# Attention with a single pass over the keys: which engines copy the transposed outputs and add them up, and where in a pair's rounds its products stand

## The reference

```
q = M @ Wq.T;  k, v = split(x @ Wkv.T + bkv)
sim = q k^T / 8, masked;  attn = softmax(sim);  out = attn @ v
out = out @ Wo.T + bo;  m = layer_norm(out + M)
z = layer_norm(relu(m @ W1.T + b1) @ W2.T + b2 + m)
```

## Time and profile before

| | |
|---|---|
| median of 3 runs | 712.91 us (712.37 to 714.04) |
| the profiled execution, device time | 711.92 us |
| its span | 710.1 us |
| mean granted TensorE clock | 0.977 of full speed |
| TensorE busy | 633.1 us, 89% |
| VectorE busy | 552.7 us, 78% |
| ScalarE busy | 363.8 us, 51% |
| GpSimd busy | 245.5 us, 35% |
| DMA | 128.37 MB, mean 181 GB/s |

### The profile page before, as it was taken

One profiled execution on the slowest core, in us unless ns is written; L12 is line 12 of the kernel. 1 busy time (PEld: TensorE's weight loads), 2 busy tenths in 40 slices (PEclk: granted clock), 3 DMA queues, 4 the chain that ended last, 5 costly groups with the idle time before them and its releaser, 6 DMA issues.

```text
span 710.1 us, 11125 instructions
## 1 busy us (share of the span) xinstructions
PE 633.1 (89%) x3382; PEld 398.3 (56%) x3382; DVE 552.7 (78%) x688; ACT 363.8 (51%) x658; POOL 245.5 (35%) x305
## 2 busy tenths in 40 slices
PE   3967999999999999998999999999998287899995
PEld 3755556555556556554565566555564144688883
DVE  5378899989998999988998999899989345433333
ACT  5355566556665566654666555566564212433332
POOL 3212552246322632264225522463221601522223
PEclk9999999999999999999999999999999699899998
DMA  7038788988898889888797998888887960023311
GB/s 281 1 77 221 201 213 208 240 204 214 206 242 205 199 220 252 201 199 203 193 239 192 215 228 228 200 215 211 199 203 197 285 166 30 30 89 95 107 64 60
DMA packets 54938, 128.37 MB, mean 181 GB/s; under 512 B 15840, under 2 KB 19424, under 8 KB 54624
## 3 DMA queue, kind: packets, MB, share of 16 engines
q1 hardware_dynamic: 44128, 101.97, 56.1%
q10 hardware_dynamic: 10752, 25.70, 13.8%
HBM read 23.80 MB, written 1.05 MB: 35 GB/s over the span
## 4 chain that ended last, share of the span: by engine, by line
PE 42%; DVE 21%; SPq 14%; issue 9%; DMA 7%; ACT 3%; ACTq 2%; DVEq 1%; POOL 1%; POOLq 0%
SPq L350 14%; DVE st L679 11%; PE tail L853 9%; PE slot L825 8%; PE slot L904 6%; PE slot L912 6%; DMA pt<-st 6%; DVE prob L669 6%; PE slot L750 5%; PE tail L750 5%; ACT prob L531 2%; ACTq L567 2%; PE tail L860 1%; DMA wq_raw<-in_wq 1%; PE slot L784 1%
## 5 line engine op out<-in xcount | busy, mean ns | idle before, releaser
L531 ACT ACTIVATE prob<-prob,negmax 128x896 f32<-128x896 f32 x224 | 233.6, 1043 | 215.1 <-DVE negmax L669 192.6
L669 DVE CUSTOM_DVE_ANT_0 prob<-slot,lower,negmax_old 128x896 f32<-128x896 f32 x224 | 248.9, 1148 | 40.6 <-PE slot L825 28.3
L679 DVE STREAM_TRANSPOSE st<-prob 128x1792 f32<-128x1792 f32 x112 | 228.4, 2040 | 15.0 <-DMA pt<-st 14.6
L853 PE MATMUL tail<-pt,val 128*64 128x512 f32 x784 | 185.2, 606 | 17.2 <-DMA pt<-st 10.8
L853 PEld LDWEIGHTS tail<-pt,val 128*64 128x64 f32 x784 | 51.7, 138 | 113.4 <-issue 105.1
L825 PE MATMUL slot<-k_hi,q_hi 64*128 64x448 f32 x448 | 95.7, 416 | 19.5 <-DVE negmax L669 16.1
L825 PEld LDWEIGHTS slot<-k_hi,q_hi 64*128 64x128 f32 x448 | 44.0, 185 | 87.0 <-issue 77.7
L825 PE MATMUL slot<-k_hi,q_lo 64*128 64x448 f32 x448 | 85.4, 366 | 0.0
L825 PE MATMUL slot<-k_lo,q_hi 64*128 64x448 f32 x448 | 84.8, 364 | 0.0
L429 POOL TENSOR_TENSOR total<-total,alpha 128x8 f32<-128x8 f32 x28 | 5.8, 206 | 199.2 <-ACT alpha L571 199.2
L442 POOL TENSOR_TENSOR k_lo<-k_raw,k_hi 128x896 fp32r<-128x896 f32 x27 | 57.1, 2114 | 3.9 <-POOL k_hi L439 0.2
(11 more groups left out here) (112 smaller groups left out, 812.6 us busy)
## 6 DMA issues: line engine op xcount, KB each, us to landing
pt<-st SPq DMA_DIRECT2D x672, 112.0 KB, 3.1
pt<-st ACTq DMA_DIRECT2D x224, 112.0 KB, 3.4
w_raw<-in_w SPq DMA_DIRECT2D x32, 256.0 KB, 2.8
x_raw<-in_x SPq DMA_DIRECT2D x13, 448.0 KB, 4.0
mask_raw<-in_mask SPq DMA_DIRECT2D x7, 448.0 KB, 4.5
mt_raw<-in_mt SPq DMA_DIRECT2D x2, 512.0 KB, 7.6
wq_raw<-in_wq SPq DMA_DIRECT2D x2, 512.0 KB, 8.2
wo_raw<-in_wo SPq DMA_DIRECT2D x1, 1024.0 KB, 5.1
```

Of the source, the lines that this page charges most:

```text
L531: nc.scalar.activation(unit, unit, ACT.Exp, bias=negmax[:, p, u:u + 1], scale=-1.0, accum_out=psumrow[:, p, u:u + 1]).then_inc(exp_done, 1)
L669: nc.vector.tensor_tensor_reduce(out=prob[:, i % 2, h].rearrange("p (b n) -> p b n", b=2), in0=slot[:, j, :, :HALF], in1=lower[:, i].rearr ...
L679: nc.vector.transpose(st[:, g].rearrange("p b k (t i) -> p k b t i", t=2)[:, :, :, t2], prob[:, i % 2].rearrange("p h (k b i) -> p (h k) b ...
L853: last = nc.tensor.matmul(outT[DH * h:DH * h + DH], val[:, val_at(i, parity ^ (p < 0)), head(p, h)], moving, start=(i == 0), stop=(i == KT ...
```

## The change

ScalarE copies `tp` into `outT_sb` after F (its part of A, a new semaphore `f_copied`), and GpSimd adds `outT_sb` to `acc`. VectorE does nothing in A. Since `outT_sb` now holds both copies in turn, C waits until the add before has been done (the last C still waits for F alone). `tp_free` waits for `f_copied` where it waited for the add. For the last two pairs, in the tail, VectorE keeps its add straight from PSUM, as a step "+".

The table ROUNDS is new: F and A stand in round 0 of every pair; W3 goes behind K; V products move to rounds 2 and 3 in pairs 0 and 1; in pair 2, V5 stands behind F and two W in round 0, and all five others of the W in round 2; ScalarE's copies of V1 to V4 stand between the two exponentials.

```
@@ -50,22 +50,22 @@
 
 
 ROUNDS = (
-    ('S E0 E1 W0 W1 W2 W3 X M1 R0',
-     'S P0 E0 V1 E1 Z K H L X B1',
-     'S E0 E1 F W4 W5 W6 C A X M0 Q',
-     'S E0 E1 V2 X B0'),
-    ('S E0 E1 W0 W1 W2 W3 X M1',
-     'S E0 V3 E1 Z K H L X B1',
-     'S E0 E1 F W4 W5 W6 C A X M0',
-     'S E0 E1 V4 X B0'),
-    ('S E0 V5 E1 W0 W1 X M1',
+    ('S F E0 A E1 W0 W1 W2 X M1 R0',
+     'S P0 E0 E1 Z K H L W3 X B1',
+     'S E0 V1 E1 W4 W5 W6 C X M0 Q',
+     'S E0 V2 E1 X B0'),
+    ('S F E0 A E1 W0 W1 W2 X M1',
+     'S E0 E1 Z K H L W3 X B1',
+     'S E0 V3 E1 W4 W5 W6 C X M0',
+     'S E0 V4 E1 X B0'),
+    ('S F E0 A E1 W0 W1 V5 X M1',
      'S E0 V6 E1 Z K H J0 L X B1',
-     'S E0 E1 F W2 W3 W4 A X R1 M0',
-     'S E0 E1 W5 W6 C X B0 J1 I'),
-    ('S E0 E1 W0 W1 W2 W3 X M1',
-     'S E0 E1 Z F K H L A X B1',
+     'S E0 E1 W2 W3 W4 W5 W6 C X R1 M0',
+     'S E0 E1 X B0 J1 I'),
+    ('S F E0 A E1 W0 W1 W2 X M1',
+     'S E0 E1 Z K H L W3 X B1',
      'S E0 E1 W4 W5 W6 C X M0',
-     'S E0 E1 N0 X B0 O'),
+     'S E0 N0 E1 X B0 O'),
 )
 
 
@@ -110,9 +110,9 @@
         out.extend([("X", b, 3), ("M", b, 1), ("B", b, 1), ("Z", b, 0)])
         out.extend([("G", 0, 0), ("T", 0, 0), ("D", 0, 0)])
         out.extend([*(("W", a, kt) for kt in range(3)), ("G", 1, 0), ("T", 1, 0), ("D", 1, 0)])
-        out.extend([*(("W", a, kt) for kt in range(3, KT)), ("C", a, 0), ("Y", 0, 0), ("F", a, 0), ("A", a, 0), ("N", a, 0)])
+        out.extend([*(("W", a, kt) for kt in range(3, KT)), ("C", a, 0), ("Y", 0, 0), ("F", a, 0), ("+", a, 0), ("N", a, 0)])
         out.extend([("Y", 0, 1), ("Y", 0, 2), ("Y", 0, 3), ("G", a, 0), ("T", a, 0), ("D", a, 0)])
-        out.extend([*(("W", b, kt) for kt in range(KT)), ("C", b, 0), ("Y", 1, 0), ("F", b, 0), ("A", b, 0), ("N", b, 0)])
+        out.extend([*(("W", b, kt) for kt in range(KT)), ("C", b, 0), ("Y", 1, 0), ("F", b, 0), ("+", b, 0), ("N", b, 0)])
         out.extend([("Y", 1, 1), ("Y", 1, 2), ("Y", 1, 3), ("G", b, 0), ("T", b, 0), ("D", b, 0)])
         out.extend([("Y", 2, t) for t in range(QT)])
     return out
@@ -218,7 +218,7 @@
         xposed = sem("xposed")
         landed = [sem(f"landed{b}") for b in range(4)]
         v_filled, v_copied = sem("v_filled"), sem("v_copied")
-        f_filled, acc_added = sem("f_filled"), sem("acc_added")
+        f_filled, f_copied, acc_added = sem("f_filled"), sem("f_copied"), sem("acc_added")
         pv_done = sem("pv_done")
         outT_copied = sem("outT_copied")
         acc_scaled = sem("acc_scaled")
@@ -432,6 +432,12 @@
                         if is_past(n, PAIRS):
                             pool.wait_ge(acc_added, n - PAIRS + 1)
                         nc.gpsimd.tensor_tensor(by_head(acc[:, own]), by_head(acc[:, own]), per_head(alpha, own), ALU.mult).then_inc(acc_scaled, 1)
+                    if kind == "A":
+                        copied, own = in_register(pool, pair_no(c, p) + 1), acc[:, p % PAIRS].rearrange("p t n -> p (t n)")
+                        pool.wait_ge(zeroed, 2)
+                        pool.wait_ge(acc_scaled, copied)
+                        pool.wait_ge(f_copied, copied)
+                        nc.gpsimd.tensor_tensor(own, own, outT_sb[:], ALU.add).then_inc(acc_added, 1)
                     if kind == "L":
                         copied, done = in_register(pool, keys_use(pair_no(c, p)) + 1), in_register(pool, pair_no(c, p))
                         pool.wait_ge(zeroed, 2)
@@ -546,10 +552,15 @@
                                              ACT.Identity, bias=bk_sb[:, p % PAIRS:p % PAIRS + 1]).then_inc(drained[KEYS_RING], 1)
                     if kind == "C":
                         act.wait_ge(pv_done, KT * (n + 1))
-                        if is_past(n, 1):
+                        if isinstance(n, int) and n == PAIRS * CHUNKS - 1:
                             act.wait_ge(f_filled, n)
+                        elif is_past(n, 1):
+                            act.wait_ge(acc_added, n)
                         nc.scalar.copy(outT_sb[:].rearrange("p (g t a i) -> p g a t i", g=2, a=QUAD, t=2),
                                        outT.rearrange("p (g a t i) -> p g a t i", g=2, a=QUAD, t=2)).then_inc(outT_copied, 1)
+                    if kind == "A":
+                        act.wait_ge(f_filled, n + 1)
+                        nc.scalar.copy(outT_sb[:], tp).then_inc(f_copied, 1)
                     if kind == "T":
                         act.wait_ge(aoT_filled, p + 1)
                         nc.scalar.activation(ao2[0][:, p], gather_bank(p), ACT.Identity, bias=bv_sb[:, p:p + 1]).then_inc(aohi, 1)
@@ -679,7 +690,8 @@
                         nc.vector.transpose(
                             st[:, g].rearrange("p b k (t i) -> p k b t i", t=2)[:, :, :, t2],
                             prob[:, i % 2].rearrange("p h (k b i) -> p (h k) b i", b=QUAD, i=LANES)).then_inc(xposed, 1)
-                    if kind == "A":
+                    if kind == "+":
+                        dve.wait_ge(acc_added, n)
                         dve.wait_ge(acc_scaled, n + 1)
                         dve.wait_ge(f_filled, n + 1)
                         own = acc[:, p % PAIRS].rearrange("p t n -> p (t n)")
@@ -801,8 +813,10 @@
                     pe.wait_ge(v_copied, KT * c + 1)
                 elif before[0] == "V":
                     pe.wait_ge(v_copied, KT * (c + before[1]) + before[2] + 1)
+                elif before[1] == PAIRS - 2 and isinstance(c, int) and c == CHUNKS - 1:
+                    pe.wait_ge(acc_added, pair_no(c, before[1]) + 1)
                 else:
-                    pe.wait_ge(acc_added, pair_no(c, before[1]) + 1)
+                    pe.wait_ge(f_copied, pair_no(c, before[1]) + 1)
 
             def body(c, sched, parity):
                 banks = bank_plan(sched)
```

## The result

The changed kernel takes 717.61 us (median of 20 runs, 713.0 to 721.53), the kernel before 710.85 us in the 20 runs beside it (708.05 to 714.18). The ratio is 1.009, 95% interval 1.007 to 1.011: **slower by 6.8 us**, where the prediction had 3.3. The profiled execution of the changed kernel took 716.73 us (span 714.9), that of the kernel before 711.92 (span 710.1).

What follows compares the result with a forecast made beforehand. TensorE (77.05 of 80 us busy) and VectorE (74.67) were near their limit, so TensorE's waits decide. Terms -3.4 + 8.0 + 0.2 - 0.85 - 0.6 = +3.3 us on the 712.91 median gave 716.2, range 708 to 722.

Steps and rivals of the forecast that it cites:

- Direction and mechanism: Whole kernel slower by 3.3 us: V5 waits for ScalarE's copy behind an exponential, and pair 2's round 3 is empty.
- Pair 2, +2.1: Pair 2 takes 21.8 us against 19.68: V5 idles 1.9 us, and the next S waits for VectorE.
- Pairs 0 and 1, +0.1 each: Pairs 0 and 1 take 18.4 us against 18.3 in the old order; TensorE sets the pace, VectorE's saving unused.
- rival B: TensorE's granted clock falls after pair 2's idle, 1.5 us a time, six times 9 us: 725 us; chance 0.08.
- Pair 3, -0.65: Pair 3: the 0.83 us wait for copy C goes and VectorE sets the pace at 17.28 us, against 18.1.
- the landing's 0.2: Pair 3, round 3: X wants pair 2's second move at 18.1, close to its landing at 17.9; 0.2 us added.
- First chunk, -3.4: First chunk, without F and A in pairs 0 to 2: 67.5 us walked anew against 70.9.
- The last chunk and the end, -1.25: Last chunk: pairs 0 and 1 +0.2, earlier M0 -0.85, one VectorE add less after the landing -0.6.
- rival C: Last chunk: later transfers find emptier queues, M1's landing shortens by 3 us, the end stays at 712.9; chance 0.17.
- GpSimd's add: The add moved to GpSimd in round 0 takes 1.21 us and costs nothing, its next readers coming over 5 us later.
- Rival D: GpSimd's add blocks one VectorE instruction per pair for 1.21 us, 24 pairs, +29 us: 745 us; chance 0.03.
- Rival A: VectorE, 0.60 us lighter per pair, runs ahead, so pair 2 stays 19.7 us: 706 us, faster; chance 0.20.

Runs made afterwards that it cites:

- order alone: The new order of rounds with VectorE still adding from PSUM, against the kernel before: 723.35 us, ratio 1.0173.
- engines alone: ScalarE's new copy and GpSimd's add in the old order, A moved up behind F, against the kernel before: 708.4 us, ratio 0.996.
- later normalising: Changed kernel with the last chunk's normalising of pair 0 moved behind X in round 1 of pair 3: 719.86 us, ratio 1.0119 to the kernel before.

## Why the prediction was right, point by point

- **Direction and mechanism: right.** Slower, since V5 waits for a copy that stands behind an exponential of its own round, and since round 3 is empty. Both holes are there with 1.79 and 1.48 us, and order alone against engines alone puts the loss on the order. W2 ahead of V5 removes half of one hole and with it nearly all of the loss. That 6.8 us came out where the sum had 3.3 is the work of several terms that erred both ways, as follows.
- **Pair 2, +2.1: right**, 1.96 without the clock. The walk from rows of the trace before was good to 0.2 us over 21.6. But the second hole had a second owner 0.87 us behind the first, GpSimd's key split, that the walk left out.
- **Pairs 0 and 1, +0.1 each: undersized.** Undisturbed ones took 18.7 to 18.8 us, where I had 18.4. Two terms failed. One is the price of W3: I gave it 0.9 us in a row and 0.9 alone, and alone it costs 0.2 more. The other is the sentence that V's move out of the K round "only levels it". I took V's 1.58 us from a row where V stands by itself and left K the rest of 4.02, 2.45. Side by side they took 1.49 and 2.52, apart 1.60 and 2.62 to 2.66. That is another 0.2, which stays when W3 goes back (18.5 us, against 18.2 in the run of engines alone); no run tested it by itself, and why neighbours cost less is open. The rows are K, W3 and S in pair 1 of chunk 2, changed kernel, and K and S of the same pair in the kernel before:

```profile
198.51 0.69 PE L762 MATMUL slot<-x_hi,wk_hi 128*128 128x448 f32 x2
...
201.15 1.08 PE L867 MATMUL tail<-pt,val 128*64 128x512 f32 x4
202.16 0.47 PE L839 MATMUL slot<-k_hi,q_hi 64*128 64x448 f32 x2
```
```profile
205.14 0.57 PE L750 MATMUL slot<-x_hi,wk_hi 128*128 128x448 f32 x2
...
207.66 0.47 PE L825 MATMUL slot<-k_hi,q_hi 64*128 64x448 f32 x2
```

F's wait, the rest of the difference, was in the walk. Ten such pairs are 3 of the missing microseconds.

- **The clock, rival B at 0.08: too small a chance, and wrong as an alternative.** It came on top of the forecast, in two of five chunks of the profile (1.6 us each, behind V5's two longest idles) and in round 0 of pair 0 in chunk 4, where an idle of 2.15 us (2.08 before) was followed by 8.50 us instead of 6.91. I had the right rows (1.97 us idle with the clock at 0.61, 1.13 without) and treated "at the edge" as "probably not"; "sometimes" was the reading. What made the two idles long, ScalarE's own move issues (0.2 and 0.6 us), wasn't in the walk at all.
- **Pair 3, -0.65: right**, -0.85, the landing's 0.2 didn't show. **First chunk, -3.4: right** in the profile, with some luck, since that stretch varies by over 1 us between kernels with the same order there; its own run has 3.4 us in the medians.
- **The last chunk and the end, -1.25: undersized**, -3.2. SP issues M1 69.2 us after the chunk's start instead of 69.7: -0.5, where I had -0.65. Behind the landing 1.0 us is saved, where I had 0.6. The missing term is M1 itself: from its first issue to the transposition that waits for it 16.3 us pass instead of 18.0. I had left that unchanged; the sign named for rival C, a landing of 8 us instead of 11, was there (7.2 behind the last issue, 11.1 before). That part of rival C was true, and it hid a part of what the pairs lost.
- **GpSimd's add: right** in that it costs nothing that shows (M1 is issued 0.3 us after SP is free). There are 26 of them, not 25 (27 less two) as the prediction counted. It takes 1274 to 1303 ns, where I had 1.21 us, and VectorE's reductions and transpositions don't feel it:

```profile
L440 POOL TENSOR_TENSOR acc<-acc,outT_sb x26: 1274/1295/1303, 86.3 to 574.7; 128x512 f32<-128x512 f32 x26
```
```profile
L680 DVE CUSTOM_DVE_ANT_0 prob<-slot,lower,negmax_old x224: 1145/1150/1153, 28.4 to 570.2; 128x896 f32<-128x896 f32 x112
```
```profile
L690 DVE STREAM_TRANSPOSE st<-prob x112: 2036/2040/2046, 33.4 to 577.1; 128x1792 f32<-128x1792 f32 x112
```

Rival D fell for these instructions. With two inputs in SBUF it can be otherwise: in the run with later normalising, VectorE's product `acc` times `inv` started 0.36 us into a GpSimd instruction (559.01 to 560.07) and took 1.25 us, the three others 0.69.

```profile
559.37 1.25 DVE L704 TENSOR_TENSOR acc<-acc,inv 128x512 f32<-128x512 f32 x1
```

Rival A, that VectorE's lead would hide V5's wait, fell too: pair 2 never took less than 21.6 us from chunk 1 on.

## What to carry to other kernels

When two engines are both over 90% busy, relief for one is worth what the other can take up: VectorE was spared 0.6 us in each of 26 pairs, 2.2% of the time. That gave 0.4% in the old order, nothing once TensorE's own waits were gone, and 0.8% in the two orders in which TensorE waited most for VectorE. In an order written by hand, ask for each step what it waits for and what stands before that on the other engine's queue; a step whose input is made in the same round is a hole, and an empty round is another. Two waits that end near each other look like one in the profile, so price the filling of a hole by the second-latest input too.

## What the runs showed of the hardware that was not expected

Idles of about 2 us on an otherwise full TensorE were sometimes, not always, followed by a granted clock of 0.50 for the work after them, 1.6 us lost a time. Before V5 one of 21 idles of 1.79 to 1.83 us had it, and all three of 2.00 to 2.41. At the start of chunk 4 idles of 2.08 and 2.13 us passed without it, one of 2.15 didn't. The two kernels with W2 ahead of V5, where V5 idled 0.9 to 1.3 us and their longest idles were 2.13 and 1.90 us, showed no drop in chunks 1 to 5 of their profiles. Whether such holes also make a kernel noisier isn't shown.

ScalarE's own move issues can hold up its next exponential: three times one began 0.12 us behind the last issue, and was 0.2, 0.4 and 0.6 us late by it.
